# The last feed-forward stage of a two-layer block: where b1, gamma and beta are applied

## The reference

```
def bitlinear(x, w, b):            # w1: 1024 x 256, w2: 256 x 1024
    xq = activation_quant(x)       # per token: round(x * 127 / max|x|), clipped, / scale
    wq = weight_quant(w)           # ternary: -1, 0, 1 times mean|w|
    return einsum('bsd,fd->bsf', xq, wq) + b

h = bitlinear(x, w1, b1)           # 1024 wide
h = gelu(h)
h = (h - mean(h)) * rsqrt(var(h) + 1e-5) * gamma + beta
return bitlinear(h, w2, b2)        # added to x
```

## Time and profile before

| | us |
|---|---|
| median of 3 runs | 528.68 |
| lowest and highest | 526.77, 528.7 |
| span of the profiled execution, first to last instruction | 521.3 |
| of it the last feed-forward stage, from about | 455 |
| PE, DVE, ACT, POOL busy over the span | 350.3, 425.2, 355.1, 163.6 |

### The profile page before, as it was taken

How to read it: one execution, slowest core, us unless ns; L and a number is a source line. 1 busy time by engine, 2 the same in 40 slices (tenths; PEclk the granted TensorE clock), 3 DMA queues, 4 the chain that set the end, 5 groups by cost and what they waited for, 6 DMA issues and landing times.

```text
span 521.3 us, 9292 instructions
## 1 busy us (share of the span) xinstructions
PE 350.3 (67%) x3330; PEld 228.7 (44%) x3330; DVE 425.2 (82%) x775; ACT 355.1 (68%) x578; POOL 163.6 (31%) x252
## 2 busy tenths in 40 slices
PE   1887654474445877588878777878788777742645
PEld 1544443331144865345545444445454444520333
DVE  2568888969989775779988898989989898567985
ACT  1454244574201455899989898999989898866761
POOL 2601243203677112012222321213221322147771
PEclk9999667688666988769999999999999999985656
DMA  8500022010000002001004010101000000000001
GB/s 270 221 2 1 1 80 80 19 63 0 0 2 1 1 0 42 1 1 22 1 4 140 2 21 2 23 0 22 3 16 7 2 1 2 2 0 1 10 21 50
DMA packets 14268, 14.83 MB, mean 28 GB/s; under 512 B 9104, under 2 KB 12816, under 8 KB 13456
## 3 DMA queue, kind: packets, MB, share of 16 engines
q1 hardware_dynamic: 13216, 13.21, 8.1%
q0 software_dynamic: 144, 0.52, 0.4%
q10 hardware_dynamic: 864, 0.53, 0.3%
HBM read 11.11 MB, written 1.05 MB: 23 GB/s over the span
## 4 chain that ended last, share of the span: by engine, by line
ACT 33%; DVE 24%; PE 20%; issue 13%; POOL 8%; DMA 2%; POOLq 0%; SPq 0%; DVEq 0%; ACTq 0%
ACT rb L642 19%; ACT rb L632 7%; POOL ra L430 3%; DVE nm L1089 2%; PE ps L1581 2%; PE ps L1566 2%; DVE rb L1009 2%; PE ps L1603 2%; POOL small L435 2%; DMA cx<-ctx_in 2%; ACT ra L694 2%; PE ps L1475 1%; PE ps L1504 1%; PE ps L1346 1%; DVE rb L1096 1%
## 5 line engine op out<-in xcount | busy, mean ns | idle before, releaser
L1089 DVE TENSOR_REDUCE nm<-ps 128x1 f32<-128x1024 f32 x128 | 155.9, 1218 | 8.0 <-PE ps L1566 4.8
L642 ACT ACTIVATE rb<-ps,eb,sq 128x1024 int16<-128x1024 f32 x128 | 161.3, 1261 | 1.2 <-POOL eb L412 1.0
L412 POOL TENSOR_SCALAR eb<-nm,sq 128x1 f32<-128x1 f32 x128 | 47.2, 369 | 181.6 <-DVE nm L1089 181.2
L1566 PE MATMUL ps<-ra,rb 128*128 128x512 bf16 x256 | 79.5, 395 | 33.2 <-ACT rb L642 32.9
L632 ACT ACTIVATE rb<-ps 128x512 f32<-128x512 f32 x128 | 84.0, 656 | 9.3 <-PE ps L1581 8.8
L1581 PEld LDWEIGHTS ps<-idb,rb 128*128 128x128 bf16 x1024 | 60.0, 97 | 63.2 <-issue 32.7
L1581 PE MATMUL ps<-idb,rb 128*128 128x128 bf16 x1024 | 78.6, 220 | 9.1 <-DVE xs L1076 4.3
L1096 DVE TENSOR_SCALAR rb<-rb 128x1024 bf16<-128x1024 int16 x128 | 53.6, 419 | 3.1 <-ACT rb L642 3.1
L1590 PE MATMUL ps<-ra,rb 128*128 128x16 bf16 x1024 | 44.4, 170 | 0.0
L1496 PE MATMUL ps<-idb,gs 128*128 128x128 bf16 x128 | 13.6, 269 | 40.0 <-DVE gs L1181 25.3
L1590 PEld LDWEIGHTS ps<-ra,rb 128*128 128x128 bf16 x1024 | 39.0, 96 | 0.2
(11 more groups left out here) (178 smaller groups left out, 677.1 us busy)
## 6 DMA issues: line engine op xcount, KB each, us to landing
stage<-w SPq DMA_DIRECT2D x2, 1024.0 KB, 4.8
rb<-ra SPq DMA_DIRECT2D x16, 128.0 KB, 2.7
rb<-wide_rows SPq DMA_DIRECT2D x1, 1536.0 KB, 6.7
xs<-x SPq DMA_DIRECT2D x4, 256.0 KB, 8.7
cx<-ctx_in SPq DMA_DIRECT2D x4, 256.0 KB, 8.8
stage<-w_gate SPq DMA_DIRECT2D x1, 1024.0 KB, 10.2
stage<-w_up SPq DMA_DIRECT2D x1, 1024.0 KB, 12.2
stage<-w_down SPq DMA_DIRECT2D x1, 1024.0 KB, 4.7
```

What stands on the lines that cost most here:

```text
L412: nc.gpsimd.tensor_scalar(eb[:, u % 3:u % 3 + 1], nm[:, u % 3:u % 3 + 1], sq[:, t, h:h + 1], LN255, ALU.mult, ALU.add).then_inc(s_bias, 1)
L642: A(esc[u % 3], bank(2 * (u % 3), 2), ACT.Exp, bias=eb[:, u % 3:u % 3 + 1], scale=sq[:, t, h:h + 1], accum_out=es[:, t % 2, h:h + 1]).then ...
L1089: V.tensor_reduce(nm[:, u % 3:u % 3 + 1], bank(2 * (u % 3), 2), AX.X, ALU.max, negate=True).then_inc(s_max, 1)
L1566: ins = M(bank(2 * (u % 3) + hf), qz[t % 2][:, h // 2, h % 2, :], kT[:, h // 2, 512 * hf:512 * hf + 512], start=True, stop=True)
```

## The change

The bias moves to TensorE. For each pair of tiles GpSimd makes two diagonal f32 matrices (bias_diagonals(j)) with one over the token's scale on the diagonal, stored where the ternary gate weights had been. widen(t) begins with two f32 matmuls of 512 columns, diagonal times the row b1, into the same banks, on which the four bf16 matmuls then add. ScalarE's gelu(t) reads PSUM, with the token's scale as the factor of the activation, so f_bias is gone. f_normalise and f_gammas are gone too: VectorE makes (h - mean) * gamma in f_centre(t) into one of two buffers and, in f_scales(t), times rstd plus beta, both as one instruction of the scalar-tensor-tensor form. The small operations of f_scales are two instead of four; the residual's factor is made by GpSimd (f_factors). fT_out moves from VectorE to ScalarE.

The loops are shorter. VectorE's round is f_scales(t-1), f_centre(t), f_to_bf(t-1), f_residual(t-2); TensorE's widen(t), transposes(t-2), down(t-3); ScalarE's gelu(t), fT_out(t-2), f_squares(t), f_round(t-1); GpSimd's f_minus_mean(t), f_rstds(t), f_factors(t-1). Three of the four pairs' diagonals are made inside the attention loop, the last one after GpSimd's f_rstds(0).

```
@@ gpsimd
+            def bias_diagonals(j):
+                pool.wait_ge(tok_inv, NP + j + 1)
+                pool.wait_ge(w_scale, W1 + 1)
...
+                tj = slice(2 * j, 2 * j + 2)
+                link(nc.gpsimd.tensor_scalar(isd[:, tj], amr[:, tj], wrec[:, W1:W1 + 1], 127.0, ALU.mult, ALU.mult))
+                for t in (2 * j, 2 * j + 1):
+                    ins = nc.gpsimd.tensor_scalar(bdiag[:, t, :], idf[:, :], isd[:, t:t + 1], 1.0, ALU.mult, ALU.mult)
+                ins.then_inc(f_diag, 1)
...
+                tl = projected_at(u - 8)
+                if tl is not None and tl % 2 == 1:
+                    bias_diagonals(tl // 2)
...
-            def f_gammas(t):
-                pool.wait_ge(f_norm, t + 1)
-                pool.wait_ge(ld_wide, 16)
-                nc.gpsimd.tensor_tensor(hw[t], hw[t], rowv["gamma"], ALU.mult).then_inc(f_gamma, 1)
@@ scalar
             def gelu(t):
-                act.wait_ge(f_h, t + 1)
-                A(hw[t], hw[t], ACT.Gelu, accum_out=fsum[:, t:t + 1]).then_inc(f_gelu, 1)
+                act.wait_ge(f_ps, t + 1)
+                act.wait_ge(f_sd, t // 2 + 1)
+                A(hw[t], bank(WIDE_BANK[t % 2], 2), ACT.Gelu, scale=sd[:, t:t + 1],
+                  accum_out=fsum[:, t:t + 1]).then_inc(f_gelu, 1)
...
-            def f_normalise(t):
-                act.wait_ge(f_rstd, t + 1)
-                A(hw[t], hw[t], ACT.Identity, bias=fnrs[:, t:t + 1], scale=frs[:, t:t + 1]).then_inc(f_norm, 1)
@@ vector
-            def f_bias(t):
...
+            def f_centre(t):
+                dve.wait_ge(f_mean, t + 1)
+                V.scalar_tensor_tensor(out=centred[t % 2], in0=hw[t], scalar=fneg[:, t:t + 1], in1=rowv["gamma"],
+                                       op0=ALU.add, op1=ALU.mult).then_inc(f_centred, 1)
...
             def f_scales(t):
-                dve.wait_ge(f_gamma, t + 1)
-                link(V.tensor_tensor(hw[t], hw[t], rowv["beta"], ALU.add))
+                dve.wait_ge(f_centred, t + 1)
+                dve.wait_ge(f_rstd, t + 1)
                 c = slice(t, t + 1)
+                link(V.scalar_tensor_tensor(out=hw[t], in0=centred[t % 2], scalar=frs[:, c], in1=rowv["beta"],
+                                            op0=ALU.mult, op1=ALU.add))
                 link(V.tensor_reduce(ymx[:, c], hw[t], AX.X, ALU.max, apply_absolute_value=True))
...
             def f_residual(t):
                 dve.wait_ge(f_dn, t + 1)
                 dve.wait_ge(x3b, t + 1)
+                dve.wait_ge(f_factor, t + 1)
...
+            for t in range(T + 3):
+                if 1 <= t <= T:
+                    f_scales(t - 1)
+                if t < T:
+                    f_centre(t)
...
+                if 1 <= t <= T:
+                    f_to_bf(t - 1)
                 if 2 <= t < T + 2:
+                    f_residual(t - 2)
@@ tensor
             def widen(t):
                 pe.wait_ge(xq_tr_sb, NP + t // 2 + 1)
+                pe.wait_ge(f_diag, t // 2 + 1)
                 if t >= 2:
-                    pe.wait_ge(f_h, t - 1)
+                    pe.wait_ge(f_gelu, t - 1)
+                else:
+                    pe.wait_ge(ld_wide, 16)
+                for hf in range(2):
+                    M(bank(WIDE_BANK[t % 2] + hf), bdiag[:, t, :], rowv["b1"][:, 512 * hf:512 * hf + 512], start=True,
+                      stop=False)
...
-            for t in range(2, T + 5):
+            for t in range(2, T + 3):
                 if t < T:
                     widen(t)
...
-                if 4 <= t < T + 4:
-                    wide_transposes(t - 4, f_bf, f_tr_sb, 2, bank16(t % 2), f_tr)
+                if t < T + 2:
+                    wide_transposes(t - 2, f_bf, f_tr_sb, 2, bank16(t % 2), f_tr)
...
-                if t >= 5:
-                    down(t - 5, W2, f_tr_sb, f_out, 2, bank(6 + (t - 5) % 2)[:, 0:D], f_dn)
+                if t >= 3:
+                    down(t - 3, W2, f_tr_sb, f_out, 2, bank(6 + (t - 3) % 2)[:, 0:D], f_dn)
```

## The result

The changed kernel takes **533.05 us** (median of 4 runs, 531.73 to 534.18), the kernel before 527.72 (4 runs, 526.11 to 528.70): a ratio of 1.0121, 95% interval 1.008 to 1.0161. It is slower, by 5.3 us in the first set and 8.25 in the second; both intervals lie above 1, and both stay under 2%. The prediction had said 536.5, between 531.0 and 544.0, so the sign and the range were right, and the value was 3.45 us too high for the first set. All medians in this document leave out two disturbed executions, of 1620 and 639 us, one of the kernel with down first and one of the reordered kernel.

The account below looks back on a forecast made before the run. It took the last feed-forward stage to be bound by ScalarE and GpSimd in turn. Six steps summed to a span of 529.1 us, 7.8 over 521.3; added to 528.68 this gave 536.5 us, range 531.0 to 544.0.

Parts of the forecast that it names:

- What bounded the kernel before: Last feed-forward stage: ScalarE and GpSimd in turn set 5.94 us a tile; VectorE's own work was 5.69.
- The new wait: Each VectorE round: the residual waits for TensorE's transposes and down after the clip, 1.6 us at full clock, 2.8 at lower.
- Step 1: Into the stage: widen(0) and widen(1) ahead of the last attention matmuls make o_scale begin 2.8 us later, at 460.3.
- Step 2: From o_scale to the first scale group: GpSimd's small LayerNorm operation waits for VectorE's centre(0), + 1.0 us.
- Steps 3 to 5: Loop rounds: round 1 takes 4.5 us, round 2 8.7, then four at 6.6 and one at 7.8.
- Step 6: End of the stage, from scale(7) through down(7) to the last residual: 9.65 us, to 526.9.
- The bias and ScalarE: f32 bias matmuls 0.90 us each at full clock, nothing exposed in rounds; ScalarE's four passes at most 5.0 us, hidden under 6.6.
- The forecast case: TensorE slow in round 2, fast for four rounds, at the lower clock after the last widen: 536.5 us, chance 0.52.
- step 4: Round 2 of the stage: TensorE comes back slow after idling, 8.7 us with the clock rising on the way, to 483.0.
- Always fast: Rival: TensorE stays at full clock in the stage, saving in steps 4, 5 and 6: 531.9 us, chance 0.22.
- always slow: Rival: TensorE at the lower clock from 463 on, rounds of 7.8 to 8.0 us: 542.5 us, chance 0.14.
- The last line of the sum: Whole kernel: span 529.1 is 7.8 us over 521.3; added to the median 528.68 this gives 536.5 us.

Follow-up runs that it names:

- the first set: First runs of the unmodified changed kernel (4 runs) against the kernel before (4 runs): 533.05 us against 527.72, ratio 1.0121.
- the second: Later repeat runs of the unmodified changed kernel (6 runs) against the kernel before (11 runs): 535.26 us against 527.01, ratio 1.0145.
- the kernel with down first: Changed kernel with TensorE's down(t-3) put ahead of transposes(t-2): 520.57 us, ratio 0.9878; run again 522.34 us, ratio 0.9923.
- the reordered kernel: Changed kernel with down ahead of transposes, widen(0) and widen(1) behind the last projection, and o_out(7), LayerNorm and centre(0) reordered: 519.59 us, ratio 0.9881.
- the experiment with the bias alone: Kernel before with only the bias by diagonal f32 matmuls on TensorE and Gelu from PSUM, loop orders untouched: 528.77 us, ratio 1.0051.
- Two kernels that take it away by two different edits: Changed kernel with TensorE's down ahead of its transposes, 520.57 us, or with VectorE's residual one round later, 522.56 us.
- the second trace: Second profiled execution of the unmodified changed kernel: span 533.3 us, stage from the last attention maximum 82.0 us; median of those runs 535.26 us.

## Why the prediction was right, and where its size was off

- **What bounded the kernel before.** Confirmed by the experiment with the bias alone: 1.27 us a tile off VectorE, period unchanged at 5.94.
- **The new wait.** Confirmed in place and price. 1.6 and 2.8 us had been put on it; VectorE's idle time in front of L1207 is 1.59 and 2.84. Two kernels that take it away by two different edits fall to a period of 4.87, where 4.9 was worked out for VectorE's own work.
- **Step 1, +2.8.** 13.6 - 10.8 = 2.8 in the second trace, counted from the last attention maximum. In the first o_scale(7) began at 461.54, not 460.3, by the slow f32 group above.
- **Step 2, +1.0.** 0.92. The way from o_scale(7) to the first scale group was 9.63, predicted 9.5.
- **Steps 3 to 5.** Rounds of 4.5, 8.5, four of 6.55 (the last of them 6.60), one of 7.80; predicted 4.5, 8.7, 6.6, 7.8. The 8.5 was predicted as TensorE's work in a row; in the trace VectorE spends 1.64 us of it waiting for the token transposes and 1.59 for down(0).
- **Step 6.** From 518.21 to the last residual's end, 527.31 + 0.48, it is 9.58, predicted 9.65.
- **The sum of the steps.** Predicted span 529.1, profiled 529.9. That they lie so near is in part luck: the slow f32 group put o_scale(7) back by 2.1 us more than step 1 had, the attention loop ended 0.9 us earlier than in the profile before (445.8 for 446.7), and the later steps were a few tenths shorter.
- **The bias and ScalarE.** 0.90 us a matmul in the fast stretches as in the earlier trace rows (1.88 for the two with the tail), and nothing exposed in the rounds. Gelu from PSUM takes 1.09 us; ScalarE's rounding has 2.08 us of idle time before it in the rounds, so ScalarE didn't bound them.
- **The clock.** The forecast case: low in step 4, 1.00 over the four rounds, low from the last widen on. "Always fast" and "always slow" were both wrong.

**The last line of the sum** is where 536.5 came out too high. It adds 7.8 to 528.68, the median of three runs; with one more run it was 527.72, which is 0.96 us of the 3.45. The other 2.5 are 7.8 less the 5.3 that the medians of the first set differ by, and no step of the sum is shown to be off by that much. In microseconds the intervals of the two ratios are 4.2 to 8.5 (0.0080 and 0.0161 of 527.72) and 5.4 to 9.9 (0.0103 and 0.0188 of 527.01); both hold the 7.8 of the sum and the 7.5 of the stages. The likely reason for the low first set is the scatter of the part ahead of the loop: two of its four executions have spans of 529.9 and 530.2 and a mean clock of 0.887, the others 532.3 and 532.4. Only the first of them has a trace, so this is argued and not shown.

The same line holds an error that cancels in the difference. I took the 7.4 us between the profiled span and the median, 528.68 - 521.3, for "launch and rest, untouched". Outside the span lie 1.8 us (526.50 - 524.7, 531.73 - 529.9). The other 5.6 lie inside the span, because the profiled execution was a fast one: its span is 3.4 and 4.3 us shorter than those of the other two traces of the kernel before, and it began its attention loop at 211.2, they at 214.5 and 215.6. Beside the experiments the kernel before was executed 59 times; seven of these have the profiled execution's mean clock of 0.866 and spans of 520.6 to 522.3, the other 52 have spans of 522.1 to 529.2. A profile and a median were set side by side that belong to executions differing by more than half the effect. Why the part ahead of the loop differs from one execution to the next is open.

## What to carry to other kernels

When loops on two engines are shifted closer together, write down for one round what each engine has just been given and what it is asked for next: if the result asked for stands behind work that was released an instruction ago, the round has a full trip through the other engine in it, and swapping two steps (or asking a round later) can remove it at no cost, as both did here. Take the time of a change from a stretch that is steadier than the whole, here the stage from the last attention maximum (74.5 or 74.6 in three traces before, 84.1 and 82.0 in two after), and look at two profiles before calling the gap between span and median a constant. A saving on an engine off the chain that sets the period, here VectorE's bias pass, was worth nothing, and taking work off TensorE can cost the clock of the work that is on the path.

## What the runs showed of the hardware that was not expected

- The part of the kernel ahead of the attention loop, the same code, ended anywhere from 211.0 to 216.3 us over twelve traces; TensorE's mean granted clock up to there was 0.81 in the two that ended at 211.2 and 211.0, 0.77 or 0.78 in the five that ended at 214.5 or later, and 0.78 to 0.80 in those between; a difference of 1% in the total can't be read from single executions.
- In the kernel without its 1.8 us of f32 matmuls a round the mean granted clock of the rounds was 0.68 where it had been 1.00, and the period 7.25 to 7.80 us where it had been 6.55.
- 34 unread matmuls kept the clock at 1.00 over the pause of the stage's head, but the clock fell later, in a round where TensorE did the same work as in the changed kernel's rounds at 1.00.
